# Three pieces per pair of tiles for the late gathers of edge rows, and a new order of the last stage

## The chip, the cores and the metric

The kernel runs on one core of one Trainium2 chip. The metric is the time of one execution on the device in microseconds (us). The kernel before takes 3802.77 us, the median of three runs (3800.56 to 3809.33).

## The reference

The input is `x`, 64 tiles of 128 nodes with 128 features each, with an adjacency matrix of 128x128 per tile and 524,288 random edges between the 8,192 nodes. Four layers run one after the other. Each is a graph step and a feed-forward step with routed experts, and each adds its result to `x`. Cut to what this change touches:

```python
x = x + L0_gnn(ln(x), adj);  x = x + L0_ffn(ln(x))        # first stage
x = x + L1_gnn(ln(x))                                     # first stage
x = x + L1_ffn(ln(x), edge_index)                         # 4 experts, gates from edges
x = x + L2_gnn(ln(x), adj);  x = x + L2_ffn(ln(x))        # 8 experts, top 2, and a shared one
x = x + L3_gnn(ln(x), adj, mask);  x = x + L3_ffn(ln(x))  # 8 experts, top 2

# L1_ffn: the gates of a node come from attention over its incoming edges
h = x @ W_gat;  e = leaky_relu(a_src[src] + a_dst[dst])
alpha = softmax of e over the edges into dst
agg = segment_sum(h[src] * alpha, dst) + b_gat
gates = softmax(top2(layernorm(agg).mean over heads))
out = sum over experts of gate * (gelu(x @ W1 + b1) @ W2 + b2)
```

The rows `h[src]` of the edges are the "edge rows": 24 numbers per edge, gathered from a table in DRAM.

## The kernel before, in words

**Stages.** The first stage computes both layers 0, the graph step of layer 1 and the four expert results of layer 1 for all nodes, and it sorts the edges by target. A short stage (`attend`) then gathers and sums the edge rows of the first 32 tiles. The last stage (`phase_c`) starts at about 2200 us. It does the edges of the other 32 tiles, the gates that come from them, and all of layers 2 and 3.

**Work in the last stage.** The 64 tiles are 16 groups of four, and two groups are a turn. Routed experts work in six batches: batches 0 to 2 are turns 0-1, 2-4 and 5-7 of layer 2, batches 3 to 5 the same of layer 3. A batch can be routed only when all its tokens are scored. Its tokens are then listed by expert in slots of 256 (23, 31 and 31 slots in the three batches of a layer). A *pass* is one slot, or half a group for the shared expert of layer 2: TensorE flips the tokens (`flip`), multiplies by the first weights (`raise`), ScalarE applies the function, TensorE multiplies by the second weights (`lower`), VectorE takes the result out of PSUM (`take`: L2428 for a slot, L2424 for the shared expert). There are 202 passes: 170 routed and 32 shared.

**Names of the steps.** These names stand in the planner's tables and in the prediction:

- `rows k` (GpSimd): piece k of the late gathers. A pair of tiles has SLOT_CUTS spans of slots, and each gather is one indirect DMA (L73) that brings one edge row for each of a tile's 128 nodes. A slot beyond the most that the pair's nodes need is skipped by a branch (L92).
- `edge b` (VectorE, one exponential on ScalarE): the sums over pair b's rows (L129 to L151). There are two buffers, so the rows of pair b wait for `edge b-2`.
- `late` (VectorE, GpSimd, ScalarE): the gates of the last 32 tiles from those sums (L160 to L164, then L2582 to L2601).
- `sum` (VectorE, L2290): adds one gated expert result of layer 1 to a turn. For turns 4 to 7 it needs `late`.
- `lift`, `enter` (VectorE and one GpSimd power, L2002): norms ahead of layer 2, for a whole turn. `adj`, `xt`, `agg`, `conv` (TensorE and ScalarE) are its graph step, `settle` (VectorE, GpSimd) adds it and norms. `f2_xt`, `f2_score` score the tokens.
- `route`, `mark`, `list`: VectorE and TensorE make the places and lists of a batch.
- `pull r` (GpSimd, L2014): two indirect DMAs that fetch the tokens of slot r. `gather`, `gather_last` (GpSimd, L2029): four indirect DMAs each, bring expert results back; `back`, `leave` (VectorE, L2324) add them.
- `ease`, `g3_xt`, `project`, `compare`, `mask`, `soften`, `pt`, `mix`, `blend`: the graph step of layer 3.

**What sets the order.** `plan_c` writes out one list of all steps. At each point it takes the step whose start, by the durations in `LONG`, less its entry in `SOONER`, is earliest. Every engine then runs its own steps in that list's order. Nothing is reordered at run time: a step that waits holds up everything behind it on its engine. GpSimd's queue holds the edge gathers, the pulls, the gathers of results and the powers of the norms.

Of the kernel before, what the change touches and what calls it, by code (L numbers as in the profile page):

```python
# [40 lines left out]
AT_BATCHES = HALF // AT_TILES  # L41
SLOT_CUTS = (0, 2, 3, 4, 5, 6, 7, 8, 9, 10, 12, 14, 20, SLOTS)
SLOTS1 = SLOTS + 1
PIECE_AT = (0, 2, 13)
PIECES_OF_PAIR = len(PIECE_AT) - 1
PLACE_BITS = 6
MOVE_AT = SRC_BITS + PLACE_BITS
# [30 lines left out]
def pair_rows(pool, env, room, pair, piece, landed):  # L78
# [8 lines left out]

    for a, z in list(zip(SLOT_CUTS, SLOT_CUTS[1:]))[PIECE_AT[piece]:PIECE_AT[piece + 1]]:
        if a == 0:
# [328 lines left out]
PE, ACTE, DVE, POOL, SP = range(5)  # L418
# [1292 lines left out]
def batch_of(turn):  # L1711
# [1 line left out]


LONG = {
    "rows": [(POOL, 8.5)], "edge": [(DVE, 3.6), (ACTE, 0.4), (DVE, 5.0)], "late": [(DVE, 7.5), (POOL, 1.2), (DVE, 9.0), (ACTE, 0.3), (DVE, 17.0)],
    "load2": [(SP, 2.0)], "sum": [(DVE, 2.8)], "lift": [(DVE, 4.0), (POOL, 1.6), (DVE, 4.2)], "enter": [(DVE, 4.0), (POOL, 1.6), (DVE, 5.6)],
    "adj": [(PE, 0.8), (ACTE, 0.6)], "xt": [(PE, 0.8), (ACTE, 0.6)], "agg": [(PE, 1.1), (ACTE, 0.6)], "conv": [(PE, 3.0)],
    "settle": [(DVE, 2.7), (POOL, 1.1), (DVE, 1.4)], "f2_xt": [(PE, 0.8), (ACTE, 0.6)], "f2_score": [(PE, 0.9), (DVE, 0.3)],
# [6 lines left out]
    "take": [(DVE, 0.5)], "store": [(SP, 0.5)]}  # L1726
LANDS = {"rows": 2.5, "load2": 6.0, "load3": 6.0, "save": 3.0, "pull": 2.5, "gather": 2.5, "gather_last": 2.5, "fetch": 5.0, "store": 3.0}
PIECES = 4
SOONER = {
    "rows": -1.0, "edge": 0.5, "late": 3.0, "save": 3.0, "blend": -2.0, "fetch": 3.0, "store": 3.0, "take": 0.5, "load2": 8.0, "adj": 0.5,  # L1730
    "xt": 2.0, "sum": -1.0, "leave": -1.0, "list": 0.5, "pull": 8.0, "enter": 0.5, "settle": 0.5, "shared": 0.5, "load3": 8.0, "gather": 2.0,
    "mask": 1.0, "soften": 0.5, "route": -1.0}


def plan_c():
# [68 lines left out]
    while True:  # L1804
        best = None
        for place, name in enumerate(rank):
# [7 lines left out]
            at = max([free[LONG["raise" if name in raises else name][0][0]]] + [done[w] + 0.1 for w in wants])  # L1814
            key = at - SOONER.get(name, 0.0)
            if best is None or (key, place) < best[:2]:
# [1020 lines left out]
```

How the kernel before makes its waits and increments, by code:

```python
    def __call__(self, ins):  # L57
        self.n += 1
        ins.then_inc(self.sem, 1)
        self.eng.wait_ge(self.sem, self.base + self.n)
# [55 lines left out]
def edge_batch(nc, dve, env, R, b, half, link, rows_landed, logits, weights, rows_used):  # L116
# [9 lines left out]
    now, g, times = slice(at, at + AT_TILES), R.rows[u], env.slot_times[:, at:at + AT_TILES, :]  # L126
    m, den, acc = env.att_max[:, now, :], env.att_den[:, now, :], env.att_acc[:, now, :]
    pen, mr, mn, den_in, sum_in = R.penalty, R.batch_max, R.new_max, R.batch_den, R.batch_sum
    link(v.tensor_scalar(pen, times, 0.0, -BIG, ALU.is_equal, ALU.mult))
    due = dve.value_load(env.rows_due[0:1, half, u, b // 2:b // 2 + 1], min_val=16 * AT_TILES * SLOT_CUTS[1], max_val=16 * SLOTS * HALF // 2)
    dve.wait_ge(rows_landed[u], due)
    link(v.tensor_tensor(e, g[:, :, :, 16:20], env.own_rows[:, now, 20:ROW].unsqueeze(2).to_broadcast(by_slot), ALU.add))
    link(v.tensor_tensor(e, e, pen.unsqueeze(3).to_broadcast(by_slot), ALU.add))
# [1 line left out]
    link(v.tensor_reduce(mr, e.rearrange("p t j h -> p t h j"), AX.X, ALU.max))  # L135
    link(v.tensor_tensor(mn, m, mr, ALU.max))
    link(v.tensor_tensor(E[:, PLACES:, :], m, mn, ALU.subtract))
    link(v.tensor_copy(m, mn))
    v.tensor_tensor(e, e, mn.unsqueeze(2).to_broadcast(by_slot), ALU.subtract).then_inc(logits, 1)
    dve.wait_ge(weights, b + 1)
    link(v.tensor_tensor(w, w, times.unsqueeze(3).to_broadcast(by_slot), ALU.mult))
    link(v.tensor_reduce(den_in, w.rearrange("p t j h -> p t h j"), AX.X, ALU.add))
```

## Time and profile before

| what | us |
|---|---|
| median of three runs | 3802.77 |
| the profiled execution | 3788.75 |
| its span | 3787.0 |
| TensorE (PE) busy | 2563.9 (68%) |
| VectorE (DVE) busy | 2557.8 (68%) |
| GpSimd (POOL) busy | 1515.9 (40%) |
| ScalarE (ACT) busy | 1331.6 (35%) |

The shares are means over stages with different limits. The last stage, from about 2200 us on, has to be read by itself. GpSimd's busy time also leaves out the 0.3 us between two indirect DMAs, so a GpSimd that issues without pause shows as 77% busy. The granted clock is the share of TensorE's full 2.4 GHz.

### The profile page before, as it was taken

What the parts mean: (1) busy time and instruction counts of PE and PEld (TensorE: products, weight loads), DVE (VectorE), ACT (ScalarE), POOL (GpSimd) and SP (SyncE); (2) the same over time, 40 slices, a digit from 0 to 9 for tenths busy, and PEclk for the clock granted to TensorE, in tenths of its full rate; (3) what the DMA queues carried; (4) which work ended last, traced back from release to release, by engine and by line L of the source; (5) the groups of instructions that cost most, each with busy time, mean ns of one, the idle gap of its engine ahead of it and who ended that gap; (6) DMA issues with size and microseconds to landing.
All of it is one profiled execution on the core that took longest, in us unless ns stands there. A gap on an engine that the chain in (4) does not pass through costs nothing. (4 is left out here: it accounts for less than half of the span.)

```text
span 3787.0 us, 44751 instructions
## 1 busy us (share of the span) xinstructions
PE 2563.9 (68%) x13000; PEld 1848.8 (49%) x13000; DVE 2557.8 (68%) x5514; ACT 1331.6 (35%) x2934; POOL 1515.9 (40%) x1359
## 2 busy tenths in 40 slices
PE   4789988898988888952000014374988888989881
PEld 2355555554545555531000013264877787878781
DVE  5988998889998995766364377756777525575312
ACT  3344444454544544420000001132323545434340
POOL 0010011000000005775277646774162357667376
PEclk8799998898988889876555556587989899989895
DMA  2000000000000014112000021261443566766683
GB/s 102 3 24 20 23 21 17 13 21 15 18 21 21 21 33 64 35 30 70 2 8 8 5 59 40 44 164 29 116 131 99 131 178 171 192 168 187 168 219 95
DMA packets 314161, 264.03 MB, mean 70 GB/s; under 512 B 102347, under 2 KB 247735, under 8 KB 313384
## 3 DMA queue, kind: packets, MB, share of 16 engines
q1 hardware_dynamic: 274824, 212.78, 19.9%
q0 software_dynamic: 39072, 48.21, 6.7%
q8 instruction: 107, 1.75, 0.2%
q14 instruction: 158, 1.29, 0.1%
HBM read 201.31 MB, written 60.82 MB: 69 GB/s over the span
## 5 line engine op out<-in xcount | busy, mean ns | idle before, releaser
L817 POOL TENSOR_TENSOR a_rstd<-a_var,minus_half 128x4 f32<-128x4 f32 x64 | 126.1, 1971 | 1292.2 <-DVE a_var L1351 1285.0
L1445 DVE TENSOR_TENSOR room<-room 128x1024 f32<-128x1024 f32 (+1 forms) x460 | 589.4, 1307 | 20.1 <-ACT room L1217 8.0
L73 POOL DMA_INDIRECT got_room<-table_dram,slot_row x426 | 447.0, 1049 | 173.2 <-issue 173.2
L2014 POOL DMA_INDIRECT c_slots<-sent,c_tokens_of_slots x340 | 349.4, 1028 | 289.7 <-PE bank L2177 202.0
L410 PE MATMUL bank<-ident,room 128*128 128x128 f32 x192 | 35.1, 326 | 631.5 <-DMA room<-in_adj 484.1
L2060 PE MATMUL bank<-c_expert_w,weights_f 128*128 128x128 f32 x2720 | 349.6, 286 | 13.6 <-DVE c_made L2428 10.1
L2248 ACT ACTIVATE weights_f<-bank,c_expert_b 128x256 f32<-128x256 f32 x680 | 278.3, 470 | 217.1 <-PE bank L2060 217.0
L2060 PEld LDWEIGHTS bank<-c_expert_w,weights_f 128*128 128x128 f32 x2720 | 342.6, 202 | 22.6 <-issue 10.2
L2060 PE MATMUL bank<-c_slots_t,c_expert_w 128*128 128x256 f32 x1360 | 343.2, 398 | 2.6 <-ACT weights_f L2248 1.7
L410 PEld LDWEIGHTS bank<-ident,room 128*128 128x128 f32 x192 | 27.3, 168 | 637.5 <-DMA room<-in_adj 485.3
L1449 DVE TENSOR_TENSOR room<-room 128x1024 f32<-128x1024 f32 x264 | 316.0, 1235 | 5.0
L839 PE MATMUL bank<-a_h1p,weights_a 128*128 128x512 f32 x544 | 272.1, 652 | 25.2 <-ACT a_dist_exp L1185 25.2
L2060 PEld LDWEIGHTS bank<-c_slots_t,c_expert_w 128*128 128x128 f32 x1360 | 259.4, 201 | 38.3 <-issue 6.2
L2428 DVE TENSOR_TENSOR c_made<-bank,c_expert_b 128x256 f32<-128x256 f32 x170 | 72.2, 424 | 264.2 <-PE bank L2060 252.9
L839 PE MATMUL bank<-a_xt,weights_a 128*128 128x512 f32 (+2 forms) x384 | 205.7, 625 | 12.1 <-ACT a_h L1147 5.2
L839 PEld LDWEIGHTS bank<-a_h1p,weights_a 128*128 128x128 f32 x544 | 110.9, 211 | 161.5 <-issue 129.4
L2029 POOL DMA_INDIRECT got_room<-made,c_places x128 | 134.9, 1054 | 45.5 <-issue 37.2
L2029 POOL DMA_INDIRECT room<-made,c_places x128 | 128.8, 1006 | 50.5 <-issue 40.1
L839 PEld LDWEIGHTS bank<-weights_a,a_h 128*128 128x128 f32 x768 | 110.0, 217 | 74.9 <-ACT a_h L1153 24.7
L839 PE MATMUL bank<-a_nmp,weights_f 128*128 128x512 f32 x256 | 134.9, 640 | 15.8 <-ACT a_h L1164 15.8
L839 PE MATMUL bank<-weights_a,a_h 128*128 128x128 f32 x768 | 120.6, 308 | 35.0 <-ACT a_conv L1196 21.3
L2002 POOL TENSOR_TENSOR ln_rstd<-ln_var,minus_half 128x4 f32<-128x4 f32 (+1 forms) x56 | 73.1, 1305 | 176.9 <-DVE ln_var L2273 176.1
(523 smaller groups left out, 5408.6 us busy)
## 6 DMA issues: line engine op xcount, KB each, us to landing
c_expert_w<-in_weights_c SPq DMA_DIRECT2D x340, 256.0 KB
made<-c_made SPq DMA_DIRECT2D x170, 128.0 KB
results_dram<-a_results SPq DMA_DIRECT2D x64, 256.0 KB, 2.1
room<-results_dram SPq DMA_DIRECT2D x16, 1024.0 KB, 7.6
c_expert_b<-in_f_b SPq DMA_DIRECT2D x170, 64.0 KB
room<-in_adj SPq DMA_DIRECT2D x32, 256.0 KB, 5.3
sent<-c_rows_to_send SPq DMA_DIRECT2D x32, 256.0 KB, 2.3
got_room<-table_dram,slot_row POOLq DMA_INDIRECT x426, 2.4
```

Source lines behind the costliest of these rows:

```text
L73: pool.indirect_dma_start(out=dst, out_offset=None, in_=env.table_dram, in_offset=bass.IndirectOffsetOnAxis(ap=index, axis=0), bounds_chec ...
L410: ins = nc.tensor.transpose(bank[0:n, j * P:(j + 1) * P], src[:, j, 0:n], ident[:, :])
L817: rstd.did(g_.tensor_tensor(st.rstd[:, :], st.var[:, :], env.minus_half[:, 0:GT], ALU.pow), what, k)
L839: return nc.tensor.matmul(out, lhsT=lhsT, rhs=rhs, start=start, stop=stop, skip_group_check=True)
L1445: ins = v.tensor_tensor(dv[:, :, j, :], sv[:, :, 0, :], sv[:, :, 1, :], (ALU.min, ALU.max)[j])
L1449: ins = v.tensor_tensor(dv(side, up), sv(0, up), sv(1, up), ALU.min if side != up else ALU.max)
L2002: nc.gpsimd.tensor_tensor(env.ln_rstd[:, 0:tiles], env.ln_var[:, 0:tiles], env.minus_half[:, 0:tiles], ALU.pow).then_inc(rstd_ready, 1)
L2014: pool.indirect_dma_start(out=XS[p.r % S_BUFS][:, j, :], out_offset=None, in_=env.sent_dram[p.q], in_offset=bass.IndirectOffsetOnAxis(ap=T ...
L2029: pool.indirect_dma_start(out=rooms[turn % 2][:, c, t, :], out_offset=None, in_=env.made_dram[q], in_offset=bass.IndirectOffsetOnAxis(ap=P ...
L2060: return nc.tensor.matmul(out, lhsT=lhsT, rhs=rhs, start=start, stop=stop, skip_group_check=True)
L2248: go(H[p.m % 2][:, c, :], U[c // 2][:, (c % 2) * SLOT:(c % 2 + 1) * SLOT], func, bias=bias).then_inc(hidden, 1)
L2428: ins = v.tensor_tensor(YB[p.r % Y_BUFS][:, :, :], y, bcast(B2[p.r % W_BUFS][:, :], [P, SLOT_TILES, D], 1), ALU.add)
```

## The change

The late gathers of a pair are cut after slots 2 and 4 instead of after slot 3, which makes three pieces. The same constant cuts the gathers of the first 32 tiles, which are issued one after the other there. In the planner's tables a piece of rows is now reckoned at 5.8 us instead of 8.5, and `SOONER` has other entries: `rows` goes from -1.0 to 2.0, and half of the names are gone. The order of the last stage, which the planner makes from these tables, changes as a whole. The work is the same: the same gathers, passes and sums.

```diff
-PIECE_AT = (0, 2, 13)
+PIECE_AT = (0, 1, 3, 13)
 PIECES_OF_PAIR = len(PIECE_AT) - 1
...
 LONG = {
-    "rows": [(POOL, 8.5)], "edge": [(DVE, 3.6), (ACTE, 0.4), (DVE, 5.0)], ...
+    "rows": [(POOL, 5.8)], "edge": [(DVE, 3.6), (ACTE, 0.4), (DVE, 5.0)], ...
...
-SOONER = {
-    "rows": -1.0, "edge": 0.5, "late": 3.0, "save": 3.0, "blend": -2.0, "fetch": 3.0, "store": 3.0, "take": 0.5, "load2": 8.0, "adj": 0.5,
-    "xt": 2.0, "sum": -1.0, "leave": -1.0, "list": 0.5, "pull": 8.0, "enter": 0.5, ...}
+SOONER = {"rows": 2.0, "edge": 0.5, "late": 3.0, "save": 2.0, "blend": -1.0, "g3_xt": 1.0, "fetch": 0.5, "store": 0.5, "take": 0.5, "load2": 5.0, "adj": 0.5}
```

Two places of the new order follow. The numbers in brackets after a form are counts. In the rows of the changed kernel the lines of the last stage are three lower (L2011 for L2014, L1999 for L2002, L2425 for L2428).

GpSimd, where the first pulls of layer 2 are issued. Before: L73 is a gather of edge rows, L81 the load of a pair's slot count, at the head of each piece, L2014 a pull, L2002 a norm's power.

```order
L81 TENSOR_LOAD pair_slots
L81 ISA x2
L73 DMA got_room<-table_dram,slot_row 128x24 x4
L92 COMPARE_AND_BRANCH
L73 DMA got_room<-table_dram,slot_row 128x24 x2
L92 UNCONDITIONAL_BRANCH
L2014 DMA c_slots<-sent,c_tokens_of_slots 128x128 x16
L2002 TENSOR_TENSOR ln_rstd<-ln_var,minus_half 128x8
L2014 DMA c_slots<-sent,c_tokens_of_slots 128x128 x6
L2002 TENSOR_TENSOR ln_rstd<-ln_var,minus_half 128x8
L81 TENSOR_LOAD pair_slots
L81 ISA x2
```

GpSimd, the same place now: the end of the last pair's last piece, then the pulls, a norm, and the power of `late` (L2038).

```order
L73 DMA got_room<-table_dram,slot_row 128x24 x12
L92 UNCONDITIONAL_BRANCH
L92 COMPARE_AND_BRANCH
L73 DMA got_room<-table_dram,slot_row 128x24 x24
L92 UNCONDITIONAL_BRANCH
L2011 DMA c_slots<-sent,c_tokens_of_slots 128x128 x2
L1999 TENSOR_TENSOR ln_rstd<-ln_var,minus_half 128x8
L2011 DMA c_slots<-sent,c_tokens_of_slots 128x128 x10
L2038 TENSOR_TENSOR got_room<-got_room,minus_half 128x32
L2011 DMA c_slots<-sent,c_tokens_of_slots 128x128 x10
```

Before, the first pull stands after the first piece of the fourteenth pair (pair 13); the second piece of that pair and pairs 14 and 15 come behind it, between pulls. Now every piece of all sixteen pairs stands ahead of the first pull.

VectorE, before `late`: the last `take` and score ahead of the last `edge`, and the start of `late` (L160).

```order
L2276 TENSOR_SCALAR c_rows_to_send<-x,ln_mv,ln_rstd 128x128 x4
L2316 COPY c_logits<-bank 128x32
L2428 TENSOR_TENSOR c_made<-bank,c_expert_b_1 128x256
L129 TENSOR_SCALAR got_room<-slot_times 128x64
L130 TENSOR_LOAD rows_due
...
L149 TENSOR_TENSOR att_acc<-att_acc,got_room 128x32
L151 TENSOR_TENSOR att_acc<-att_acc,got_room 128x32
L160 TENSOR_SCALAR att_den<-att_den 128x128
```

VectorE, the same place now: `enter 2` (L2273 to L2277), the take of the first routed pass, the last `edge`, `late`.

```order
L2273 TENSOR_SCALAR room<-room,ln_mv,ln_rstd 128x128 x8
L2276 TENSOR_TENSOR room<-room,spread 128x1024
L2277 TENSOR_TENSOR room<-room,spread 128x1024
L2425 TENSOR_TENSOR c_made<-bank,c_expert_b_0 128x256
L129 TENSOR_SCALAR got_room<-slot_times 128x64
L130 TENSOR_LOAD rows_due
...
L149 TENSOR_TENSOR att_acc<-att_acc,got_room 128x32
L151 TENSOR_TENSOR att_acc<-att_acc,got_room 128x32
L160 TENSOR_SCALAR att_den<-att_den 128x128
```

Before, 24 takes and the settles of groups 0 to 7 stand ahead of `late` on VectorE. Now 9 takes and the settles of groups 0 to 3 do.

## Rows read from the trace of the kernel before

**Rows 1.** Windows of TensorE: stretch, length, busy (instructions), granted clock, DMA share, GB/s.

```profile
2463.00:2510.00 47.00, 38.01 (x217) 0.86 0.60 162
2510.00:2656.50 146.50, 79.00 (x486) 0.77 0.29 73
2656.50:2742.00 85.50, 81.71 (x538) 0.98 0.47 129
2742.00:2912.00 170.00, 145.18 (x948) 0.92 0.48 128
...
3506.00:3711.00 205.00, 181.95 (x1208) 0.92 0.73 193
3711.00:3787.00 76.00, 0.00 (x0) 0.53 0.27 73
sum 1324.00, PE 1036.42; mean PE 115.16
```

**Rows 2.** Waits of TensorE, 2657 to 3711 us: total us, times, longest.

```profile
PE bank L2060 <- DVE c_token_hot L2410: 55.6, 28, 3.0
PE bank L2060 <- DVE c_lane_total L2371: 20.9, 5, 4.9
```

**Rows 3.** Timeline of TensorE, 2350 to 2657 us: start, length, what, idle before.

```profile
2352.15 1.97 PE L410 MATMUL bank<-ident,room 128*128 128x128 f32 x8 [51.40 <-DVE room L2280]
...
2466.72 0.69 PE L2177 MATMUL bank<-ident,c_slots 128*128 128x128 f32 x2 [17.89 <-DMA c_slots<-sent,c_tokens_of_slots]
...
2656.54 1.09 PE L410 MATMUL bank<-ident,room 128*128 128x128 f32 x4 [36.09 <-DVE c_logits L2316]
```

**Rows 4.** Windows of the edge gathers alone (L73, GpSimd).

```profile
2391.50:2462.70 71.20, 55.08 (x52) 0.55 0.24 50
2495.00:2511.70 16.70, 12.65 (x12) 1.00 0.57 154
2516.90:2525.30 8.40, 6.65 (x6) 0.92 0.20 38
2536.70:2555.00 18.30, 14.16 (x14) 0.99 0.92 271
2556.70:2565.10 8.40, 6.58 (x6) 0.51 0.08 7
2566.70:2596.30 29.60, 22.89 (x22) 0.93 0.17 31
```

**Rows 5.** Timeline of GpSimd at its waits and at the first pull.

```profile
2294.69 0.99 POOL L73 DMA_INDIRECT got_room<-table_dram,slot_row  x1 [9.07 <-issue]
...
2327.29 1.67 POOL L2002 TENSOR_TENSOR ln_rstd<-ln_var,minus_half 128x8 f32<-128x8 f32 x1 [3.09 <-DVE ln_var L2273]
...
2391.83 1.00 POOL L73 DMA_INDIRECT got_room<-table_dram,slot_row  x1 [6.77 <-issue]
...
2462.76 1.00 POOL L2014 DMA_INDIRECT c_slots<-sent,c_tokens_of_slots  x1 [0.30 <-issue]
```

**Rows 6.** Timeline of VectorE: the first routed take, the last edge, `late`.

```profile
2475.13 0.42 DVE L2428 TENSOR_TENSOR c_made<-bank,c_expert_b 128x256 f32<-128x256 f32 x1 [3.81 <-PE bank L2060]
...
2610.53 0.20 DVE L129 TENSOR_SCALAR got_room<-slot_times 128x64 f32<-128x64 f32 x1
...
2620.78 0.23 DVE L160 TENSOR_SCALAR att_den<-att_den 128x128 f32<-128x128 f32 x1
...
2654.84 1.22 DVE L2601 TENSOR_REDUCE gates<-got_room 128x32 f32<-128x1024 f32 x1
```

**Rows 7.** Timeline of VectorE, two takes of routed passes in a row.

```profile
3573.47 0.42 DVE L2428 TENSOR_TENSOR c_made<-bank,c_expert_b 128x256 f32<-128x256 f32 x1 [3.31 <-PE bank L2060]
3577.21 0.42 DVE L2428 TENSOR_TENSOR c_made<-bank,c_expert_b 128x256 f32<-128x256 f32 x1 [3.31 <-PE bank L2060]
```

**Rows 8.** Timeline of TensorE, from a turn's first `xt` to the end of its `conv`.

```profile
2500.09 1.09 PE L410 MATMUL bank<-ident,room 128*128 128x128 f32 x8 [1.35 <-DVE room L2280]
...
2511.36 0.48 PE L2060 MATMUL bank<-rows,ones 1*128 1x128 f32 x2
```

**Rows 9.** Timeline of GpSimd, the gathers behind the last store.

```profile
3714.43 1.00 POOL L2029 DMA_INDIRECT room<-made,c_places  x1 [2.81 <-issue]
...
3776.25 1.00 POOL L2029 DMA_INDIRECT room<-made,c_places  x1 [0.30 <-issue]
```

**Rows 10.** Windows of VectorE: stretch, length, busy (instructions), granted clock, DMA share, GB/s.

```profile
2656.50:2742.00 85.50, 62.82 (x234) 0.98 0.47 129
```

More of the change, by code:

```diff
@@ L1715 @@
 LONG = {
-    "rows": [(POOL, 8.5)], "edge": [(DVE, 3.6), (ACTE, 0.4), (DVE, 5.0)], "late": [(DVE, 7.5), (POOL, 1.2), (DVE, 9.0), (ACTE, 0.3), (DVE, 17.0)],
+    "rows": [(POOL, 5.8)], "edge": [(DVE, 3.6), (ACTE, 0.4), (DVE, 5.0)], "late": [(DVE, 7.5), (POOL, 1.2), (DVE, 9.0), (ACTE, 0.3), (DVE, 17.0)],
     "load2": [(SP, 2.0)], "sum": [(DVE, 2.8)], "lift": [(DVE, 4.0), (POOL, 1.6), (DVE, 4.2)], "enter": [(DVE, 4.0), (POOL, 1.6), (DVE, 5.6)],
@@ L1728 @@
 PIECES = 4
-SOONER = {
-    "rows": -1.0, "edge": 0.5, "late": 3.0, "save": 3.0, "blend": -2.0, "fetch": 3.0, "store": 3.0, "take": 0.5, "load2": 8.0, "adj": 0.5,
-    "xt": 2.0, "sum": -1.0, "leave": -1.0, "list": 0.5, "pull": 8.0, "enter": 0.5, "settle": 0.5, "shared": 0.5, "load3": 8.0, "gather": 2.0,
-    "mask": 1.0, "soften": 0.5, "route": -1.0}
+SOONER = {"rows": 2.0, "edge": 0.5, "late": 3.0, "save": 2.0, "blend": -1.0, "g3_xt": 1.0, "fetch": 0.5, "store": 0.5, "take": 0.5, "load2": 5.0, "adj": 0.5}
 def plan_c():
```

## The prediction

> **What bounds the kernel now.** The two versions have the same instructions in all stages but the last, so I read the last stage by itself, first in the windows of TensorE. From 2656.5 to 3711 us it is busy 919 of 1054.5 us (the sum 1036.4 less 38.0 and 79.0), so it is close to the limit there [rows 1]. Ahead of that it is not: in 2510 to 2656.5 it does 79 us of work in 146.5, at a granted clock of 0.77 [rows 1]. The timeline of TensorE says what it waits for in the early part: 51.4 us for VectorE's norm, 17.9 us for the first pulled tokens, and 36.1 us behind a VectorE that is busy with `late` [rows 3]. The windows of the edge gathers name the engine behind those waits: from 2391.5 to 2462.7 GpSimd issues 52 gathers without a pause, and the first pull is queued behind them [rows 4, 5]. Last I read the end. TensorE stops at 3711, and GpSimd then issues 48 gathers of results from 3714.4 to 3776.3 that need the last store [rows 1, 9]. This tail of 76 us is the same in both orders: 12 pieces of `gather_last` have to wait for the last store in either.
>
> So the end is the time at which TensorE has done all its work, plus a fixed 76 us. TensorE's work does not change. What the change can move is TensorE's idle time.
>
> **The change part by part.**
>
> *Three pieces instead of two.* No gather is added. Each late pair has one more load of its slot count (L81), 16 in all, and there are 16 more in the stage before. In the 52 gathers of [rows 4] there are seven pieces, each with such a load, and the mean from start to start is 70.9 / 52 = 1.36 us, of which 1.06 is busy and 0.3 is the gap that stands between any two indirect DMAs [rows 4, 5]. The loads cost nothing visible. I take 0 for the 32 new ones; the upper bound is 0.3 us for each, 10 us, the lower bound is 0, since a load removes nothing.
>
> The cut also lets the first two slots of a pair go out while `edge` or a norm is still awaited. GpSimd's waits in the early part that such a piece can fill are 9.1, 3.1 and 6.8 us [rows 5]. I followed the new order piece by piece with these durations. The 9.1 us shrink since `edge 3` now stands ahead of `settle 1` and the takes, the 6.8 us go, but other waits of 3 to 5 us come up since a piece now stands ahead of a norm on GpSimd and VectorE waits for that norm. Net I take 3.5 us earlier; bounds 0 and 19 us (all three).
>
> *The first pull.* Before it stands behind 13 pairs and one piece, now behind all 16 pairs. The order shows what moves ahead of it: the second piece of pair 13 and pairs 14 and 15, which are the 12 + 6 + 14 + 6 + 22 = 60 gathers that the trace shows between 2495 and 2596.3 [rows 4]. At 1.36 us they are 81.8 us; by their own windows they are 81.4. One norm's power (`lift 2`) also moves ahead, 1.9 us. The first pull goes from 2462.8 to 2462.8 + 81.8 + 1.9 - 3.5 = 2543.0 us. TensorE has nothing to do in that time except marks: its next routed pass needs the pull, and its next groups need `enter 2`, whose power now stands behind the first pull.
>
> *`late`.* VectorE's row is now: take of the first routed pass, last `edge`, `late`. The take comes 12.4 us after the first pull's start (2475.13 - 2462.76) and lasts 0.4; the last edge is 2610.53 to 2620.78, 10.2 us; `late` is 2620.78 to 2656.1, 35.3 us [rows 5, 6]. So `late` ends at 2543.0 + 12.4 + 0.4 + 10.2 + 35.3 = 2601.3 instead of 2656.1 us, 55 us earlier.
>
> *What TensorE has done by then.* Before, when `late` ends, passes up to 25 are lowered and groups 4 to 7 are through their graph step. Now passes up to 10 are lowered (the next needs a take that stands behind `late`) and groups 4 and 5 are through. TensorE is behind by 15 passes and by the rest of four groups. A pass takes 3.73 us where nothing but TensorE limits it [rows 7]; 15 are 56 us. The graph step of two groups takes 11.7 us [rows 8]. Scores, flips of the adjacency and the bias rows of the shared passes I put at 12 us, an estimate from their counts at the durations of neighbouring matmuls. Sum 80 us. Bounds: TensorE's whole busy time in the stretch in which it did this work is 79.0 us, and some 8 us of passes ahead of 2510 belong to it as well, 87 [rows 1]; with the waits in between counted as unavoidable it would be 95; with the estimated 12 left out, 68.
>
> What the row shows of the clock: in that stretch TensorE was granted 0.77 of full speed after its waits, against 0.98 in the next [rows 1]. The Trainium skill, "TensorE: Matmul & The Clock Gate", Part 1, says that the throttled state is the default and that activity releases it. By that rule the moved work, which now comes in one stretch behind `late`, would run at the full clock, and 80 us would stand; by the row, at a clock of 0.77 as before, it would be the 87.
>
> *Behind `late`.* Before, TensorE idles 1054.5 - 919.4 = 135 us between `late` and its end. Of this, 55.6 + 20.9 = 76.5 us are the five routings (marks that VectorE makes, and the lane totals) [rows 2]. The new order has the marks of batches 1, 2, 4 and 5 in the same kind of row, with at most one or two passes between them, so I leave these. The other 58.5 us are many small waits. VectorE stays under TensorE: behind `late` it is busy 63 us where TensorE is busy 82 [rows 1, 10], and the moved work (four settles, a `lift` and `enter`, four sums, 15 takes) is, by an estimate from such steps, some 50 us for 80 of TensorE. I take the 135 as unchanged. Bounds: half of the 58.5 filled by the passes that are now in store, -29; or the moved 80 us done at the efficiency of the stretch 2742 to 2912, 145.2 of 170 us [rows 1], +14.
>
> *Sum, against the profiled execution.* `late` ends 55 us sooner, TensorE has 80 us more to do from there, the rest is equal: +25 us. Its time of 3788.75 us becomes 3814. That execution was 14 us faster than the median of the runs, which is what will be compared, so I add the difference to the median: 3802.8 + 25 = 3828 us.
>
> **The rivals.**
>
> *The early `late` decides (faster).* Place: TensorE between 2742 and 3711 us. `late` frees VectorE and the sums of turns 4 to 7 55 us earlier, so TensorE holds more passes in store whenever VectorE or GpSimd is slow, and the small waits go. If 45 of the 58.5 us are filled, the sum is 25 - 45 = -20 us: 3783 us. It decides from 33 us filled. For it: GpSimd has no edge gathers left after 2543, 82 us of its queue gone. Against it: TensorE at 82 of 85.5 us behind `late` has no room in the first stretch [rows 1], and the new order is behind by six passes at every later routing, so it has not more of them ready, only more left.
>
> *Both halves meet (no change).* The gathers' waits all go (first pull at 2527 instead of 2543) and some 10 us of small waits are filled: 25 - 16 - 10 = 0: 3803 us.
>
> *VectorE or GpSimd joins in (much slower).* Behind `late` GpSimd has 14 pulls more to issue (28 indirect DMAs at 1.3 us, 37 us) and VectorE all norms of groups 4 to 7. If a norm's power then stands behind pulls that wait for TensorE, the 80 us take 94, and one more wait of some 6 us comes with it: +45 us: 3848 us. For it: the powers and pulls share one queue, and each wait holds VectorE. Against it: VectorE is busy 63 of the 85.5 us behind `late` before, about as much as it will be [rows 10].
>
> *The change doesn't do what it says.* If the third piece were all, the time would be the same within its 0 to 10 us; the order says it is not all.
>
> **How the numbers follow.** The forecast has 0.55, much slower 0.15, no change 0.15, faster 0.15. Within 0.2% is 7.6 us either way, about what a measurement of this kernel can tell from no change. So slower 0.70, same 0.15, faster 0.15. The forecast's own range, with the bounds of the first pull (-16, +5), the work (-12, +15) and the rest (-29, +14), is 3805 to 3848. With the other cases taken in until 2 in 10 are left out: 3798 to 3850.
>
> **What would show it.** Right: the last edge gather ends near 2541 us, the first pull starts at 2543 (2530 to 2550), TensorE idles over 130 us between its last marked batch and this pull's tokens except for marks, `late` ends near 2601, and TensorE's last matmul is 25 us later than 3711 with 76 us behind it. Wrong: the first pull before 2525, more than 10 passes taken by the end of `late`, or TensorE idle for less than 105 us between `late` and its end. If `late` ends at 2600 and the time is still not longer, the step that failed is the 135 us.

## The result, and the profile after

| | before | after |
|---|---|---|
| median of 11 runs, us | 3803.03 | 3815.42 |
| lowest to highest, us | 3800.56 to 3810.16 | 3804.09 to 3819.89 |
| ratio, 95% interval | | 1.0031 [1.0022, 1.0039] |
| profiled execution, us | 3788.75 | 3804.09 |
| its span, us | 3787.0 | 3802.3 |

The change makes the kernel some 12 us slower, where +25 was forecast; the profiled executions differ by 15.3 us. A profile shows one execution: that of the kernel before was 14.3 us below the median of its runs, that of the kernel after 11.3 below. Windows of TensorE in the kernel after, cut at the stage's first late gather, at the end of `late` and at TensorE's last matmul (stretch, length, busy and instructions, granted clock, DMA share, GB/s):

```profile
2205.20:2603.10 397.90, 133.30 (x650) 0.61 0.19 47
2603.10:3720.70 1117.60, 992.87 (x6514) 0.92 0.62 164
3720.70:3802.30 81.60, 0.03 (x1) 0.52 0.25 68
```

The kernel before, cut at the same three events:

```profile
2203.70:2656.10 452.40, 203.82 (x1176) 0.70 0.28 70
2656.10:3710.90 1054.80, 919.37 (x5988) 0.91 0.61 161
```

These five rows are the whole balance, and it closes:

| us | before | after | difference |
|---|---|---|---|
| start of the stage | 2203.7 | 2205.2 | +1.5 |
| from there to the end of `late` | 452.4 | 397.9 | -54.5 |
| TensorE busy behind `late` | 919.4 | 992.9 | +73.5 |
| TensorE idle behind `late` | 135.4 | 124.7 | -10.7 |
| tail behind its last matmul | 76.1 | 81.6 | +5.5 |
| sum | | | +15.3 |

`late` is ready 54.5 us sooner, and TensorE has 73.5 us more to do from there. Read in idle time: ahead of `late` TensorE idles 452.4 - 203.8 = 248.6 us before and 397.9 - 133.3 = 264.6 after; behind it, 10.7 us less.

The first pull is where it was forecast. The timeline of GpSimd shows it behind the last edge gather (start, length, what, idle before), and the one of TensorE shows what the wait for it costs:

```profile
2543.33 1.01 POOL L73 DMA_INDIRECT got_room<-table_dram,slot_row  x1 [0.30 <-issue]
2544.64 1.00 POOL L2011 DMA_INDIRECT c_slots<-sent,c_tokens_of_slots  x1 [0.30 <-issue]
```

```profile
2548.52 0.69 PE L2174 MATMUL bank<-ident,c_slots 128*128 128x128 f32 x2 [95.98 <-DMA c_slots<-sent,c_tokens_of_slots]
```

Before, this wait was 17.9 us [rows 3]. Behind the 96 us the stretch to the end of `late` ran at a granted clock of 0.81 and the one behind `late` at 0.98:

```profile
2548.50:2603.10 54.60, 33.84 (x174) 0.81 0.17 37
2603.10:2735.00 131.90, 125.81 (x846) 0.98 0.59 167
```

VectorE ends `late` at 2601.89 + 1.22 = 2603.1 us, against 2656.1 [rows 6]:

```profile
2601.89 1.22 DVE L2598 TENSOR_REDUCE gates<-got_room 128x32 f32<-128x1024 f32 x1
2603.25 0.88 DVE L2425 TENSOR_TENSOR c_made<-bank,c_expert_b 128x256 f32<-128x256 f32 x2
```

Waits of TensorE behind `late`, 2604 to 3720 us (total us, times, longest). The marks (`c_token_hot`) and the lane totals together are 4.0 us below [rows 2]:

```profile
PE bank L2057 <- DVE c_token_hot L2407: 54.3, 28, 2.8
PE bank L2057 <- DVE c_lane_total L2368: 18.2, 5, 5.8
PE bank L410 <- DVE room L2273: 5.2, 2, 4.8
PE bank L410 <- DVE room L2277: 1.1, 1, 1.1
```

The waits for `room`, the normed rows that VectorE hands to TensorE, have fallen more, from 11.9 us in all to 6.3. Before, 2657 to 3711 us:

```profile
PE bank L410 <- DVE room L2276: 8.0, 2, 7.3
PE bank L410 <- DVE room L2280: 3.9, 3, 3.0
```

The tail is new. In the kernel after, VectorE's timeline at its end, and then the queue of SyncE there:

```profile
3720.34 4.42 DVE L2321 SCALAR_TENSOR_TENSOR x<-room,c_place_weights,x 128x128 f32<-128x128 f32 x16 [5.59 <-DMA room<-made,c_places]
3724.79 0.88 DVE L2425 TENSOR_TENSOR c_made<-bank,c_expert_b 128x256 f32<-128x256 f32 x2
```

```profile
3708.13 7.01 SPq L1974 DMA_DIRECT2D made<-c_made  x4
3724.78 0.38 SPq L1989 DMA_DIRECT2D out<-x  x1
3725.24 1.77 SPq L1974 DMA_DIRECT2D made<-c_made  x2
```

The closing step of batch 4 (its `leave`: 16 sums of results on VectorE, then the first store of x on SyncE) now stands ahead of the last two takes and stores. Before, the store of x stands behind all stores of c_made:

```profile
3701.26 10.59 SPq L1977 DMA_DIRECT2D made<-c_made  x4
3717.80 0.38 SPq L1992 DMA_DIRECT2D out<-x  x1
```

So the last 48 gathers, which began at 3714.43 [rows 9], begin at 3729.71 now, 9.0 us behind TensorE's end instead of 3.5:

```profile
3729.71 1.00 POOL L2026 DMA_INDIRECT room<-made,c_places  x1 [10.97 <-issue]
```

### The profile page after: what moved, and what is told of

Its sections match the earlier page's. It is cut to its first block and busy times, and to the rows that moved or that the text cites. A ratio compares the mean times of both kernels' runs of the same rounds, so it can differ in the third digit from the quotient of the medians.

```text
span 3802.3 us, 44845 instructions
## 1 busy us (share of the span) xinstructions
PE 2567.4 (68%) x13000; PEld 1849.1 (49%) x13000; DVE 2557.6 (67%) x5514; ACT 1330.7 (35%) x2932; POOL 1518.6 (40%) x1359
## 5 line engine op out<-in xcount | busy, mean ns | idle before, releaser
L817 POOL TENSOR_TENSOR a_rstd<-a_var,minus_half 128x4 f32<-128x4 f32 x64 | 126.1, 1971 | 1294.7 <-DVE a_var L1351 1287.6
L73 POOL DMA_INDIRECT got_room<-table_dram,slot_row x426 | 445.9, 1047 | 177.9 <-issue 177.9
L2011 POOL DMA_INDIRECT c_slots<-sent,c_tokens_of_slots x340 | 353.3, 1039 | 283.1 <-PE bank L2174 196.8
L2425 DVE TENSOR_TENSOR c_made<-bank,c_expert_b 128x256 f32<-128x256 f32 x170 | 72.1, 424 | 278.3 <-PE bank L2057 260.4
L2235 ACT ACTIVATE c_slots_t<-bank 128x256 f32<-128x256 f32 x170 | 65.3, 384 | 269.1 <-PE bank L2174 265.5
L1999 POOL TENSOR_TENSOR ln_rstd<-ln_var,minus_half 128x4 f32<-128x4 f32 (+1 forms) x56 | 73.1, 1305 | 197.1 <-DVE ln_var L2270 192.7
L2174 PE MATMUL bank<-ident,c_slots 128*128 128x128 f32 x340 | 69.7, 288 | 113.7 <-DMA c_slots<-sent,c_tokens_of_slots 104.7
```

What stands on the lines that cost most here:

```text
L73: pool.indirect_dma_start(out=dst, out_offset=None, in_=env.table_dram, in_offset=bass.IndirectOffsetOnAxis(ap=index, axis=0), bounds_chec ...
L817: rstd.did(g_.tensor_tensor(st.rstd[:, :], st.var[:, :], env.minus_half[:, 0:GT], ALU.pow), what, k)
L1999: nc.gpsimd.tensor_tensor(env.ln_rstd[:, 0:tiles], env.ln_var[:, 0:tiles], env.minus_half[:, 0:tiles], ALU.pow).then_inc(rstd_ready, 1)
L2011: pool.indirect_dma_start(out=XS[p.r % S_BUFS][:, j, :], out_offset=None, in_=env.sent_dram[p.q], in_offset=bass.IndirectOffsetOnAxis(ap=T ...
L2174: ins = nc.tensor.transpose(XB[:, j * P:(j + 1) * P], XS[p.r % S_BUFS][:, j, :], env.ident[:, :])
L2425: ins = v.tensor_tensor(YB[p.r % Y_BUFS][:, :, :], y, bcast(B2[p.r % W_BUFS][:, :], [P, SLOT_TILES, D], 1), ALU.add)
```

## The experiments

Twelve runs, on three chips; each ratio is against the kernel before, run on the same chip beside it. Experiments 1 to 4 share one chip, where the kernel before takes 3796.27 us; experiment 5 and the first runs of 8 and 9 share the second (4002.03); the others share the third (3793.07). In a profile the balance above is made again. The measured balances come first, so that each experiment can point at its line (us; "taken" is the number of passes that VectorE has taken by the end of `late`).

| | taken | stage start to end of `late` | busy behind | idle behind | tail | ratio [95%] |
|---|---|---|---|---|---|---|
| before | 24 | 452.4 | 919.4 | 135.4 | 76.1 | |
| after | 9 | 397.9 | 992.9 | 124.7 | 81.6 | 1.0031 [1.0022, 1.0039] |
| cut only | 24 | 452.2 | 920.4 | 136.1 | 75.8 | 0.9996 [0.9974, 1.0018] |
| order only | 9 | 392.2 | 1012.7 | 122.9 | 81.0 | 1.0042 [1.0020, 1.0065] |
| rows at -1.0 | 27 | 468.7 | 911.3 | 138.2 | 81.0 | 1.0011 [0.9989, 1.0033] |
| leave behind the takes | 9 | 398.9 | 996.5 | 126.1 | 82.0 | 1.0031 [1.0008, 1.0054] |
| rows at -4.0 | 39 | 525.7 | 871.5 | 167.5 | 80.7 | 1.0170 [1.0156, 1.0184] |
| before, leave early | 24 | 451.3 | 920.6 | 131.3 | 84.9 | 1.0036 [1.0023, 1.0050] |
| before, marks spread | 24 | 454.1 | 925.8 | 112.3 | 75.8 | 0.9930 [0.9917, 0.9944] |
| all three | 39 | 530.3 | 863.9 | 157.4 | 75.8 | 1.0088 [1.0074, 1.0102] |

The profiles of the second chip are left out, since TensorE's idle time there is another (207.3 us behind `late` in the kernel after). The columns come from one execution each, the ratios from medians, and one execution can lie up to 14 us off its median. So differences of a few us between two balances are read only where several profiles agree.

**1. The cut alone.** The order of the kernel before, with each late pair's first piece cut in two.

```diff
-PIECE_AT = (0, 2, 13)
+PIECE_AT = (0, 1, 2, 13)
+PLANNED_PIECES = 2
...
+        if what == "rows":
+            b, second = divmod(k, 2)
+            order += [("rows", 3 * b + 2)] if second else [("rows", 3 * b), ("rows", 3 * b + 1)]
```

> The order of the kernel before, with every pair's rows in three pieces instead of two, the first two of which stand next to each other, so that each engine has the same gathers, pulls and sums in the same order. Only the 32 extra loads of a slot count and their branches are new. Theory (the order did it): 0 us, within 2. Rival (the third piece costs by itself): up to 0.3 us for each load, +10 us.

Measured: 3795.84 us beside 3796.27, and behind the start of the stage the balance is that of before within 1.0 us. A third piece costs nothing that can be seen; by the interval a cost of more than 7 us is excluded. The cut tried here is not at the place of the changed kernel's (behind slots 2 and 4).

**2. The new order alone.** The kernel before, two pieces, with the new `SOONER`.

```diff
-SOONER = {"rows": -1.0, "edge": 0.5, "late": 3.0, "save": 3.0, "blend": -2.0, ...}
+SOONER = {"rows": 2.0, "edge": 0.5, "late": 3.0, "save": 2.0, "blend": -1.0, ...}
```

> The kernel before, two pieces per pair, with only SOONER exchanged for that of the changed kernel. In its order all rows again stand ahead of the first pull and 9 takes ahead of late. Theory (the order did it, by putting the edges first): like the changed kernel, +12 us against before, within 5; the first pull at 2544 to 2552 us, late at 2603 to 2612, after which TensorE has some 1115 us to its end. Rival (the cut is needed for the loss): within 4 us of before.

Measured: 3813.58 us, +17, where 12 was expected within 5. The slowdown comes from the order, without the cut. Its windows show the same shape as the kernel after, `late` early and much left behind it:

```profile
2207.70:2599.90 392.20, 121.98 (x578) 0.59 0.20 48
2599.90:3735.50 1135.60, 1012.69 (x6586) 0.91 0.61 161
```

**3. One number of the order back.** The kernel after, with `rows` at -1.0: 18 pulls stand ahead of the last piece of edge rows again.

```diff
-SOONER = {"rows": 2.0, ...
+SOONER = {"rows": -1.0, ...
```

> The changed kernel with one number of its table back: rows -1.0 in SOONER instead of 2.0. The first pull stands behind 38 of 48 pieces again and 18 pulls ahead of the last rows; 27 takes stand ahead of late, 9 in the changed kernel, 24 in the one before. Routings 4 and 5 and the end are those of the changed kernel. Theory (a ledger of TensorE: late comes later by the pulls' time on GpSimd, 18 x 2.6 = 47 us and some norms and waits, 55 to 60 in all, but TensorE has 19 passes, 71 us, and two groups, some 20 us, less to do behind it; small waits take 10 to 20 back): 12 to 20 us faster than the changed kernel, so within 8 of before, with late near 2660. Rival (an early late is worth as much as it comes sooner): slower than the changed kernel by 20 us or more.

Measured: 3802.59 us, some 11 less than the order alone and 8 less than experiment 4, which keeps the new place of the pulls, all on one chip. That is less than the 12 to 20 that were expected, and `late` ends at 2678.8 us, not near 2660. What is left against before is inside the interval, and the tail is still the long one (81.0). Counted from the start of the stage, `late` is 70.8 us later than in the kernel after, 81.6 us of work have gone from behind it, and 13.5 us of idle time have come, where 10 to 20 less were expected (windows of TensorE, cut at the same events):

```profile
2210.10:2678.80 468.70, 224.59 (x1270) 0.69 0.27 68
2678.80:3728.30 1049.50, 911.28 (x5894) 0.90 0.61 162
```

These single executions don't show the gain of the medians. The profiled execution here (3811.02 us) is 8.4 us above its median; against the profile of experiment 4, on the same chip (3811.91), it is 0.9 us shorter where the medians differ by 8.5. That the pulls' place costs time rests on the medians; the balances show what is exchanged, not the net of it.

**4. The leave of batch 4, first try.** The kernel after, with this step moved behind the last take; by the edit it stays ahead of the last two stores on SyncE.

```diff
+    at, last = order.index(("leave", 4)), order.index(("take", len(passes) - 1))
+    if at < last:
+        order.insert(last, order.pop(at))
```

> The changed kernel with one step moved on VectorE: leave 4 (16 operations, 4.4 us) stands behind the last two takes, as in the kernel before, instead of ahead of them. Theory: in the changed kernel the last take waits for leave 4, so the last store and the 48 gathers behind it start late; the tail behind TensorE's last matmul goes from 81.6 to 76 us, and the time falls by 4 to 6 us against the changed kernel. Rival (the tail is set by GpSimd's gathers ahead of it, gather_last 16 to 19): no change, and GpSimd issues without a pause up to the first gather of the last batch.

A miss: 3811.05 us, ratio as after, tail 82.0. VectorE's last take is no longer held, but SyncE's queue is, and GpSimd's first gather of the last 48 waits for it:

```profile
3716.08 6.52 SPq L1977 DMA_DIRECT2D made<-c_made  x4
3733.19 0.38 SPq L1992 DMA_DIRECT2D out<-x  x1
3733.61 1.80 SPq L1977 DMA_DIRECT2D made<-c_made  x2
```

```profile
3738.12 0.99 POOL L2029 DMA_INDIRECT room<-made,c_places  x1 [11.86 <-DMA made<-c_made]
```

TensorE ended at 3728.2; the store of x waits for VectorE's sums until 3733.2, and the two stores behind it that the last gathers need wait with it. Two queues carried the same order, and I had moved the step on one.

**5. The same step behind the stores, too.**

```diff
+    leave, stored = order.index(("leave", 4)), order.index(("store", sum(p.r is not None for p in passes) - 1))
+    if leave < stored:
+        order.insert(stored, order.pop(leave))
```

> The changed kernel with the closing step of batch 4 (its leave) moved behind the last store of a pass on VectorE and on SyncE. Theory (the closing step's write to memory stands on SyncE ahead of the two last stores of c_made, holds them until VectorE has made its operand, and so holds the gathers of batch 5 behind them): the tail from TensorE's end to the span's end goes back from 81.6 to about 76 us, GpSimd's wait before the last batch's first gather from 11.0 to 6 us, and the time falls 4 to 6 us against the changed kernel beside it. Rival (the tail is longer because a gather or store itself is slower in that place): the tail stays at 81 to 82 us and the time is the same within 2 us.

3999.61 us beside 4002.03 (1.0001 [0.9975, 1.0028]). This shows nothing of the step, because on this chip the tail is not long in the changed kernel either. The kernel after, once more on the same chip:

> The changed kernel unchanged, so that the others of this call stand beside it on one chip: 1.003 of the kernel before, +10 to +15 us; late at 2603, tail 81 to 82 us.

4004.60 us, 1.0013 [0.9987, 1.0038], tail 75.7: neither the 10 to 15 us nor the long tail that were expected. TensorE ends so late there that VectorE's sums are done before it: the store of x goes out at 3911.1, TensorE's last matmul ends at 3912.6.

```profile
3911.10 0.38 SPq L1989 DMA_DIRECT2D out<-x  x1
3911.56 1.95 SPq L1974 DMA_DIRECT2D made<-c_made  x2
```

**6. The mirror.** The kernel before, with nothing but this step moved ahead of the last two takes and stores.

```diff
+    taken = order.index(("take", len(passes) - 2))
+    order.insert(taken, order.pop(order.index(("leave", 4))))
```

> The kernel before with the closing step of batch 4 moved ahead of the last two takes on VectorE and so ahead of the last two stores of c_made on SyncE, as it stands in the changed kernel; nothing else is moved. Theory (this placing alone lengthens the tail where VectorE's closing step ends after TensorE's last pass): the tail from TensorE's end to the span's end grows from 76 to 80 to 82 us, and the time by 4 to 6 us (1.001 to 1.0015). If on this chip TensorE ends later than the closing step's operand, as it did on the chip of the second call (tail 75.7 us with the changed kernel), the tail stays at 76. Rival (the long tail comes with the order of the passes, not with this step): the tail stays at 76 us even though the row of the store of x stands ahead of the last two of c_made and after TensorE's end.

Measured: 3804.18 us beside 3793.07, +11, twice what was expected; tail 84.9 instead of 76.1. The sums wait for gathers of batch 4 and end 7.5 us after TensorE (3709.1), and both queues hold what stands behind them until then:

```profile
3712.22 4.41 DVE L2326 SCALAR_TENSOR_TENSOR x<-room,c_place_weights,x 128x128 f32<-128x128 f32 x16 [9.12 <-DMA room<-made,c_places]
3716.67 0.88 DVE L2430 TENSOR_TENSOR c_made<-bank,c_expert_b 128x256 f32<-128x256 f32 x2
```

The step's place alone lengthens the tail. The profile shows 8.8 us of it, the medians 11 (by the interval 9 to 19); the difference is no larger than what one execution lies off its median.

**7. More pulls ahead than before.** The kernel after, with `rows` at -4.0: 23 pulls ahead of the last piece, 39 passes taken by the end of `late`.

> The changed kernel (three pieces) with the due time of rows set to -4.0 in SOONER, where it has 2.0: by the order 23 pulls then stand ahead of the last piece of edge rows and 39 passes are taken ahead of late, against none and 9 in the changed kernel, 16 and 24 before, 18 and 27 at -1.0. Theory (each pull ahead of the last rows costs late some 3.9 us and buys 4.5 us of TensorE's work that is else done behind late, as the run at -1.0 measured against the changed kernel: late 70.9 us later for 18 pulls, 81.6 us less work behind it, 13.5 us more idle time): late near 2693, 135 us less work behind late than the changed kernel (about 858), idle time behind late 143 to 150, and a time 0.995 to 0.999 of the kernel before. Rival (the passes ahead of late are no longer in time that is else idle, since TensorE is full there by now): late comes 10 us or more later than that, or its idle time ahead of late does not fall, and the time is 1.001 to 1.005.

The largest miss: 1.0170. I had drawn a straight line through two points. `late` ends at 2734, 41 us later than the line gave. One part of it is in GpSimd's timeline and in the windows of TensorE:

```profile
2568.35 1.00 POOL L2011 DMA_INDIRECT c_slots<-sent,c_tokens_of_slots  x1 [1.42 <-PE bank L2174]
2569.66 1.00 POOL L2011 DMA_INDIRECT c_slots<-sent,c_tokens_of_slots  x1 [0.30 <-issue]
2572.08 1.00 POOL L2011 DMA_INDIRECT c_slots<-sent,c_tokens_of_slots  x1 [1.42 <-PE bank L2174]
```

```profile
2440.00:2560.00 120.00, 108.60 (x683) 0.93 0.38 99
2560.00:2590.00 30.00, 30.00 (x208) 0.99 0.83 200
2590.00:2734.00 144.00, 23.31 (x142) 0.59 0.13 26
```

From 2560 to 2590 the pulls wait for TensorE, and the two gathers of one pull take 3.73 us (2572.08 - 2568.35), the length of a pass, while edge rows stand behind them. The larger part is elsewhere. From the start of the stage to the last edge gather GpSimd takes 57 us more than in experiment 3. It waits 18 us more for TensorE in the pulls, but 35 us more for VectorE ahead of the powers of the norms, which stand in the same queue; here and then in experiment 3 (total us, times, longest):

```profile
POOL ln_rstd L1999 <- DVE ln_var L2270: 79.0, 14, 11.0
```

```profile
POOL ln_rstd L1999 <- DVE ln_var L2270: 44.1, 12, 11.4
```

Then the pulls are used up, since the first batch has 23 slots. The last 74 gathers of edge rows go out in one run from 2589.6 to 2688, and TensorE does 23 us of work in 144. It has nothing left until the groups that need `late` have been summed and normed, and of this one wait 36 us lie behind `late`:

```profile
2769.96 1.97 PE L410 MATMUL bank<-ident,room 128*128 128x128 f32 x8 [149.82 <-DVE room L2277]
```

So 36 of the 167.5 us of idle time in the table are this wait. An early pull pays only while others are left to lay between the gathers that follow.

**8. The marks spread.** The kernel before; the matmuls of a mark, of batches 1 to 5, come one after each raise of a pass, and VectorE makes the operand one mark ahead.

```diff
+            if what == "raise" and marks:
+                out.append(marks.pop(0))
+                if made:
+                    out.append(made.pop(0))
```

> The kernel before, with the marks of batches 1 to 5 no longer in one block: TensorE's product of a mark comes one after each raise of a pass, and VectorE's operand for it one mark earlier. Theory (behind late the idle time of TensorE is in the routings, most of it 28 waits of about 2 us for VectorE's c_token_hot, each a round trip that a pass laid between would cover): the waits for c_token_hot fall from 55.6 us to 5 to 20, TensorE's idle time behind late from 135 to 95 to 115 us, and the time falls 20 to 40 us. Rival (VectorE is as full as TensorE there, so a pass laid between delays VectorE's takes by what it saves TensorE): c_token_hot goes, waits for other operands of VectorE come up in its place, and the time is within 8 us of before.

3976.83 us beside 4002.03, 0.9922 [0.9894, 0.9950]. Its profile is of another chip than that of the kernel before. On the third chip:

> The kernel before with the marks spread, a second time, beside the others of this call: 0.990 to 0.995 of the kernel before; waits of TensorE for c_token_hot 5 to 20 us (55.6 before).

3767.99 us beside 3793.07, 0.9930. TensorE's idle time behind `late` falls from 135.4 to 112.3 us and its work grows by 6.4. With the other terms the balance gives 13.6 us less than the profile of before, the medians 25: the one profiled execution is 7.1 us above its median, that of before below. The waits for marks are not as low as expected, 34.8 against 55.6 us:

```profile
PE bank L2108 <- DVE c_token_hot L2458: 34.8, 16, 6.0
PE bank L2108 <- DVE c_lane_total L2419: 18.6, 5, 4.9
```

The waits for the marks fall by 20.8 us of the 23.1. The rival wanted other operands of VectorE in their place; none came up by more than 2.5 us. This version beats both kernels.

**9. Spread marks in the changed kernel, then all three.** First the kernel after with experiment 5 and 8 together:

> The changed kernel with the leave of batch 4 behind the last store and the marks spread as in the other. If the two idle costs are independent of where the passes stand, its gain against the changed kernel is that of the spread kernel before plus the 4 to 6 us of the tail: 24 to 46 us; if the spread is worth nothing, 4 to 6 us.

3980.31 us, 0.9957 [0.9932, 0.9982]: 24 us less than the kernel after beside it (4004.60), as much as the spread gave before (25). The marks' gain is the same in either order, as far as these intervals tell (some 10 us either way). Whether it adds to the order's loss isn't shown there, since the order alone cost nothing that could be measured on that chip. Then the same with `rows` at -4.0:

> The changed kernel with the due time of rows at -4.0, the closing step of batch 4 behind the last store, and the marks spread among the passes. If the three gains add: 0.992 from the marks, 0 to 0.004 from more passes ahead of late, so 0.988 to 0.993 of the kernel before. If passes laid ahead of late are then missing as cover behind it, 0.992 or more.

3826.34 us, 1.0088, where 0.988 to 0.993 was expected if the gains add. It carries the loss of experiment 7 (`late` at 2736.4). Beside that run it is 32 us faster, and its tail is 75.8 instead of 80.7: here, on a chip where the tail was long, the step behind the stores takes it back, though together with the marks. The step behind the stores alone was never measured where the tail is long.

## Why the prediction was right in sign and too large

- **Three pieces cost nothing:** right within 7 us (experiment 1). Experiment 2 shows that the order loses without them too.
- **The first pull at 2543.0:** 2544.6, of which 1.5 is the later start of the stage. The 60 gathers at 1.36 us carry it; that the gathers' waits would shrink by 3.5 us net, with bounds of 0 and 19, was a guess that happened to fit.
- **`late` 55 us sooner, at 2601.3:** 54.5 and 2603.1. The 9 takes ahead of it are as the order has them.
- **80 us more for TensorE behind `late`:** 73.5. This term was 6.5 too large. The 12 us that were an estimate were the soft part; with the 56 and 11.7 taken as they are, some 6 of them are there. The stretch behind `late` ran at a granted clock of 0.98, not at the 0.77 of [rows 1], so the 87 us that the row of before gave would have been further off. This agrees with the Trainium skill, "TensorE: Matmul & The Clock Gate", Part 1, as cited in the prediction.
- **135 us of idle time behind `late`, unchanged:** this step failed. It was 124.7. I had named the direction in the rival "the early `late` decides", but priced it at all or nothing; that rival would have needed 33 us. The profiles agree: 122.9 to 126.1 in three with 9 passes taken by the end of `late`, 131.3 to 136.1 in three with 24. Of the 10.7 us, 5.6 are waits for `room` and 4.0 waits for marks and lane totals; the others are small and go both ways. That each pass in store covers a part of such a wait is not shown. With 27 and 39 passes taken the idle time is 138.2 and 167.5, and without the 36 us of experiment 7 the last is 131.5, no more than with 24.
- **The tail of 76 us, the same:** this step failed too, by +5.5, and I had a row for it. I counted the gathers behind the last store, and not what stands ahead of that store on its queue. Experiment 6 shows it, and experiment 4 that moving the step on one queue isn't enough.

The misses partly cancel: 25 - 6.5 (work) - 10.7 (idle) + 5.5 (tail) + 0.5 (`late`) + 1.5 (start) = 15.3. The medians say 12.4. So the forecast of 3828 us was 12.6 us off, and the rival "both halves meet" with its 3803 about as far (12.4). Of that rival the first half, the gathers' waits, did not come, and the second did. "Much slower" with 3848 was further off. The lower end of the stated range, 3805, doesn't follow from the three bounds beside it: added up they give 3771 to 3862, and as a root of squares 3793 to 3849.

Why the order loses, in one exchange: a pull of two gathers (2.6 us of GpSimd) laid ahead of the last edge rows gives TensorE a pass of 3.73 us [rows 7] in time that is else idle, and it makes `late` later. The change took 16 pulls back: `late` came 54.5 us sooner, 3.4 us for each, and 73.5 us more work lay behind it, passes and steps of groups together. Experiment 3 put 18 ahead again and exchanged 70.8 us of `late` for 81.6 us of work. By the medians it took back 8.5 of the 14.8 us that experiment 4 loses on that chip, and what is left has the long tail in it. Experiment 7 goes past the point where pulls are left, and loses 1.7%.

## What to carry to other kernels

Before an engine's work is put ahead of another's on a shared queue, draw up the balance at the event it hastens: how much sooner the event is, how much work is then left behind it, and what becomes of the idle time behind it. Make it from more than one execution where the net is as small as their scatter. Do not stretch the rate found between two orders beyond the point where the cheap item runs out. When a step is moved, look at each queue that carries it, the store queue at the very end above all: one store that waits for a slow operand holds the stores that the last gathers need.

## What was not expected of the hardware

The second chip ran the same kernel before at 4002.03 us, where the others gave 3803.03, 3796.27 and 3793.07. A take is no slower in the changed kernel there (424 ns in both profiles), nor is an edge gather (1049 against 1047 ns), and the mean granted clock is 0.803 against 0.809. TensorE is: over the same 6514 instructions behind `late` it was busy 1047.8 us instead of 992.9, and a matmul with the first expert weights took 418 ns in the mean instead of 398. It idled 207.3 us instead of 124.7, and a wait leads the list that the other profile does not have, one for nothing that the profile shows:

```profile
PE bank L2057 <- issue: 58.4, 51, 3.5
PE bank L2057 <- DVE c_token_hot L2407: 51.8, 25, 3.0
PE bank L2057 <- DVE c_lane_total L2368: 25.2, 5, 7.7
PE bank L2057 <- ACT weights_f L2245: 23.8, 21, 5.8
```

The cause is open. It matters for the method: absolute times of two chips do not compare, and the ratio of the change was 1.0013 [0.9987, 1.0038] there and 1.0031 on another. The tail was not lengthened there, which would account for such a difference, but the intervals overlap and don't show one. A cost that hangs on which of two engines ends last can be there on one chip and not on the next.
